# Graph network on 50,000 nodes: target low digits from ScalarE's sign function, late row gathers, run marks stored as rows

## The chip, the cores and the metric

The kernel runs on 1 core of one Trainium2 chip. The metric is device time in microseconds (us) of one launch. The same inputs and outputs hold for both kernels.

## The reference, cut to what matters

```python
def reference(x, src, dst, edge_attr_17, ...):          # x [50000, 96], 25000 edges, sorted by dst
    def L0(x, edge_attr, ...):
        h = relu(edge_attr @ W1.T + b1)
        w = h @ W2.T + b2
        agg = segment_sum(w * x[src], dst, N)
        return relu(x @ Ws.T + bs + agg @ Wn.T + bn)
    def L1(x):                                           # 10 times
        deg_row = maximum(segment_sum(ones, src, N), 1)
        deg_col = maximum(segment_sum(ones, dst, N), 1)
        w = rsqrt(deg_row[src] * deg_col[dst])
        out = segment_sum(out[dst] * w[:, None], src, N) * 0.9 + x * 0.1
    def L2(x):                                           # 16 times, with self-loops
        h = 0.9 * segment_sum(norm * h[row], col, N) + 0.1 * x
    def L3(x):                                           # two graph convolutions with prelu
        ...
    x = layernorm(x + L0(x)); x = layernorm(x + L1(x))
    x = layernorm(x + L2(x)); x = layernorm(x + L3(x))
```

`layernorm` has no affine part. The edges' degrees by source and by target, and the place of each edge in an order by source, depend on the indices alone and are worked out at the start.

## The kernel before

Edges lie in 196 tiles of 128, four tiles to a group, 49 groups of 512 edges (`NT`, `U`, `NGP`, `GE`). The program is a row of blocks with a boundary of all engines between them: `histograms` (L580), `node_records` (L1292), `rank_edges` (L917), `prepare` (L1379), and then `passes` (L1753), the power iteration, the smoothing and the two convolutions. The change touches the first four and the head of the power iteration.

**`histograms`** does three things per group of four tiles, side by side. It counts the edges of each node: a node's number is split in a high digit (196 values) and a low digit (256 values), VectorE writes one-hot rows of each digit (`onehots`, L737 and L738, for target and source, so 16 operations a group), and TensorE multiplies them into two tables in its accumulators (`count`, L812), targets as they come, sources behind the group. ScalarE copies the source table before each group (L908, `snap`) and VectorE stores what rounding lost (`remainder`, L744). Secondly it works out the edge weights: TensorE turns the edge attributes (L820), ScalarE copies them (`copy_edges`, L880), TensorE multiplies (`hide`, L825), ScalarE adds the bias and rectifies (`rectify`, L886), and TensorE multiplies again (`weigh`, L834). Thirdly POOL gathers the rows of x by source (L665, four gathers a group, 196 in all), at most two groups beyond the last that has landed and paced by `remainder`, and VectorE multiplies them by the weights (`gate`, L751). SyncE stores the snapshots and copies x.

The order of ScalarE in the loop is written by hand: snapshot of the counts up to group g, `rectify(g - 1)`, `copy_edges(g)`. TensorE's is: the target counts of tile 0, `weigh(g - 1)`, the target counts of tile 1, the turning of group g's edges, tile 2, tile 3, `hide(g)`, then the source counts of the group. All of it is in order on each engine, so `weigh` holds up what is behind it.

**`node_records`** sums the two tables over the nodes (a running sum, L1348) and writes a record for each node; POOL makes three constants there. **`rank_edges`** gathers records by source (POOL, L988) and by target, places each edge in the order by source (VectorE, L1067 and L1076), sums the gated rows of each run of equal targets (L1125, with the marks of the runs loaded by SyncE and inverted at L1134), and does the first layer. **`prepare`** scatters the edges' records into the order by source, reads them back, works out where runs of equal sources begin (`cont`, L1679 to L1681) and stores these marks to `mask_s` (L1487, four numbers of each partition). Its POOL program ends with four gathers of x rows for the power iteration (`fetch_own`, L564); the first pass fetches the rest.

Of the kernel before, what the change touches and what calls it, by code (L numbers as in the profile page):

```python
# [20 lines left out]
P = 128  # L21
# [28 lines left out]
OWN_FIRST, OWN, OWN_SOON = 124, 8, 4  # L50
# [5 lines left out]
PACE = 2  # L56
# [368 lines left out]
class Program:  # L425
# [130 lines left out]

    def fetch_own(self, pool, tiles):
# [22 lines left out]
    def histograms(self):  # L580
# [4 lines left out]
        with ExitStack() as s:  # L585
# [13 lines left out]
            def part(rows, cols):  # L599
# [26 lines left out]
            const, cleared, onehot, counted, rounded, split, joined = (  # L626
                self.local(f"hist_{n}") for n in ("const", "cleared", "onehot", "counted", "rounded", "split", "joined"))
# [17 lines left out]
            def _(pool):  # L645
# [13 lines left out]
                for g in range(NGP):  # L659
                    if g >= AHEAD_GROUPS:  # L660
                        pool.wait_ge(self.fills(g - AHEAD_GROUPS), self.full(g - AHEAD_GROUPS))
                    if g >= PACE:
                        pool.wait_ge(split, g - PACE + 1)
                    for t in range(g * U, (g + 1) * U):
                        nc.gpsimd.indirect_dma_start(  # L665
                            out=T[:, t * D:(t + 1) * D], out_offset=None, in_=i["x"],
                            in_offset=bass.IndirectOffsetOnAxis(ap=self.src_i[:, t:t + 1], axis=0),
                        ).then_inc(self.fills(g), 16)

            @block.sync  # L670
            def _(sp):
                def load_edge(n):
                    if n >= RE:
                        sp.wait_ge(G["turned"], n - RE + 1)
                    rows = min(GE, E - n * GE) // U
                    sp.dma_start(ea[n % RE][0:rows, :],
                                 i["ea"][n * GE:n * GE + rows * U, :].rearrange("(p u) c -> p (u c)", u=U)
                                 ).then_inc(el[n % RE], 16)

                sp.wait_ge(blank, 3)  # L680
# [40 lines left out]
            def _(dve):  # L721
# [25 lines left out]
                def gate(n):  # L747
                    dve.wait_ge(G["product"], n + 1)
                    dve.wait_ge(self.fills(n), self.full(n))
                    c = slice(n * GD, (n + 1) * GD)  # L750
# [25 lines left out]
                for x in (self.src_i, self.dst_i, next_i):  # L776
                    v.memset(x[:, :], int(PAD)).then_inc(blank, 1)
                link(v.memset(zero[:, :], 0.0))
# [13 lines left out]
                digits(1, self.key_d)  # L792
                dve.wait_ge(const, 4)
# [15 lines left out]
            def _(pe):  # L809
# [63 lines left out]
            def _(act):  # L873
# [13 lines left out]

                act.wait_ge(spread, 1)
# [11 lines left out]
                a_.activation(self.w2[0:D, :], self.bank[5][0:D, 0:D], ACT.Copy).then_inc(set_, 1)  # L900
                for g in range(NGP):
# [6 lines left out]
                    a_.activation(snap[g % SK][:, 0:2 * HW], hist[0], ACT.Copy).then_inc(rounded, 1)  # L908
                    if g:
# [7 lines left out]
    def rank_edges(self):  # L917
# [6 lines left out]
        with ExitStack() as s:  # L924
            def tmp(name, shape, dt=fp32):
# [27 lines left out]
                self.local(f"run_{n}") for n in ("led", "started", "turned", "scanned", "back", "kept"))  # L953
            follows_in = [self.local(f"run_follows{k}") for k in range(2)]
# [13 lines left out]
            def _(pool):  # L968
# [7 lines left out]
                                        fill=0.0, base=0, pattern=[[-1, P]], channel_multiplier=1).then_inc(const, 1)  # L976
                for k, (index, of_, into, groups) in enumerate((
                        (self.src_i, self.meta, self.ms, NGP), (self.dst_i, self.both_t, rows_in, BOTH_FIRST))):
                    if k:
                        pool.wait_ge(met, 16 * MET)  # L980
                    for g in range(groups):
                        q = k * NGP + g
                        if q >= AHEAD_GROUPS:
                            pool.wait_ge(self.fills(q - AHEAD_GROUPS), self.full(q - AHEAD_GROUPS))
                        if q * NT // (NGP + BOTH_FIRST) > PACE * U:
                            pool.wait_ge(nears, q * NT // (NGP + BOTH_FIRST) - PACE * U)
# [69 lines left out]
            def _(dve):  # L1056
# [60 lines left out]

                def run_totals(m):
# [14 lines left out]
                dve.wait_ge(led_in, 16)  # L1133
                v.tensor_scalar(starts, led, -1.0, 1.0, ALU.mult, ALU.add).then_inc(started, 1)  # L1134
                low_digits(0)
                for k in range(LAST):
                    for t in (2 * k, 2 * k + 1):
# [19 lines left out]
            def _(pe):  # L1157
# [34 lines left out]
                def turn_runs(m):  # L1192
                    r = NGP - 1 - m
                    if m >= 2:
# [97 lines left out]
    def node_records(self):  # L1292
        nc = self.nc
        with ExitStack() as s:
# [10 lines left out]
            off = tmp("off", [HP, 1])  # L1305
# [6 lines left out]
            def _(pool):  # L1312
# [7 lines left out]
                               allow_small_or_imprecise_dtypes=True).then_inc(const, 1)  # L1320
            @block.tensor
# [19 lines left out]
            def _(dve):  # L1341
# [3 lines left out]
                for k in range(2):  # L1345
                    dve.wait_ge(turned, k + 1)
                    link(nc.vector.tensor_copy(deg[k][:, :], self.bank[4 + k][0:HP, :]))
                    link(nc.vector.tensor_tensor_scan(out=cum[:, :], data0=ones[:, :], data1=deg[k][:, :], initial=0.0,  # L1348
                                                      op0=ALU.mult, op1=ALU.add))
                    dve.sem_inc(totals, 1)  # L1350
# [1182 lines left out]
```

## Time and profile before

| | us |
|---|---|
| runs | 8792.99, 8794.96 (median), 8802.09 |
| profiled execution | 8794.6 |
| its span, first to last instruction | 8792.5 |
| mean granted clock of TensorE | 0.663 |
| POOL busy in the span | 6478.6 (74%) |
| TensorE busy | 5522.7 (63%) |
| VectorE busy | 4914.3 (56%) |
| ScalarE busy | 2041.9 (23%) |

The profile is of one execution. Engines are PE (TensorE), PEld (its weight loads), DVE (VectorE), ACT (ScalarE), POOL (GpSimd) and SP (SyncE); a `q` behind a name is the engine's queue of instructions, and L744 is line 744 of the kernel. Idle time is put down to what ended it. The granted clock is given as a share of full speed.

In the profiled execution `histograms` runs from 0 to 287 us, `node_records` from 287 to 310, `rank_edges` from 310 to 843, `prepare` from 843 to 1184, and the power iteration follows.

### The profile page before, as it was taken

To read this page: it belongs to the slowest core of one execution; us is meant where nothing else is said; L and a number is where in the kernel's file an instruction comes from. 1 tells how busy PE (TensorE), PEld (TensorE's weight loads), DVE (VectorE), ACT (ScalarE), POOL (GpSimd) and SP (SyncE) were. 2 spreads that over 40 slices of the span, in tenths; PEclk is the share of its full clock that TensorE was granted. 3 is DMA by queue.
4 is the path that set the end of the run, shared out by engine and by line. 5 is a ranking of instruction groups with operands and counts; after the bars stand their busy time and mean duration, and the time that the engine had idled before them with its cause. 6 is when DMAs were issued, how large, how long until landed. Compare 5 with 4: busy or idle time off the path is not lost. (4 is left out here: it accounts for less than half of the span.)

```text
span 8792.5 us, 112510 instructions
## 1 busy us (share of the span) xinstructions
PE 5522.7 (63%) x24034; PEld 4418.1 (50%) x24034; DVE 4914.3 (56%) x12173; ACT 2041.9 (23%) x5604; POOL 6478.6 (74%) x6812
## 2 busy tenths in 40 slices
PE   7676835555555543347777777777776667766643
PEld 6565723333333332226666666656555555655533
DVE  7688736555556566645555555544444444465544
ACT  2355832111111113533111111100000000065433
POOL 6666767777777777677777777777777777777777
PEclk9777855555555555557877777777667666666555
DMA  7665564444444433323444444433333333333211
GB/s 143 130 163 155 148 128 128 113 113 112 113 112 117 115 106 109 110 70 113 121 112 115 114 114 113 113 105 101 96 99 98 98 98 98 103 94 88 81 45 37
DMA packets 955827, 954.11 MB, mean 109 GB/s; under 512 B 426114, under 2 KB 846716, under 8 KB 955046
## 3 DMA queue, kind: packets, MB, share of 16 engines
q1 hardware_dynamic: 696366, 602.87, 22.8%
q0 software_dynamic: 217408, 320.06, 16.7%
q10 hardware_dynamic: 41370, 23.99, 1.1%
q8 instruction: 195, 3.19, 0.1%
q14 instruction: 488, 4.00, 0.1%
HBM read 565.09 MB, written 409.02 MB: 111 GB/s over the span
## 5 line engine op out<-in xcount | busy, mean ns | idle before, releaser
L1996 POOL DMA_INDIRECT l_g<-tab,marks x3094 | 2922.8, 945 | 951.4 <-issue 870.6
L2214 DVE TENSOR_TENSOR_SCAN l_w<-l_m,l_w,bank 96x512 f32<-96x512 bf16 x1248 | 1591.4, 1275 | 2620.5 <-PE bank L2028 2610.7
L2028 PE MATMUL bank<-ident,l_g 128*96 128x128 f32 x5030 | 1165.3, 375 | 1627.7 <-DMA l_g<-tab,marks 914.3
L1996 POOL DMA_INDIRECT l_g<-tab,XM x1740 | 1648.2, 947 | 541.4 <-issue 476.3
L2028 PEld LDWEIGHTS bank<-ident,l_g 128*96 128x96 f32 x5030 | 755.0, 171 | 2073.9 <-DMA l_g<-tab,marks 1030.3
L2048 PEld LDWEIGHTS bank<-ident,l_w 96*128 96x128 f32 x6272 | 1603.7, 328 | 327.9 <-issue 256.4
L2048 PE MATMUL bank<-ident,l_w 96*128 96x96 f32 x6272 | 1508.9, 403 | 10.2 <-DVE l_w L2214 10.2
L2039 PE MATMUL bank<-XM,ident 128*128 128x384 f32 x1568 | 921.4, 681 | 0.0
L2118 ACT ACTIVATE T<-T,marks 128x96 f32<-128x96 f32 x196 | 57.0, 362 | 1967.1 <-DVE T L2239 1966.7
L309 PE MATMUL bank<-tail_xt,v 96*96 96x500 f32 (+1 forms) x298 | 275.7, 1026 | 319.9 <-ACT tail_xt L304 319.9
L420 ACT ACTIVATE tail_y<-bank,tail_of,tail_sc 125x96 f32<-125x96 f32 (+1 forms) x596 | 208.2, 429 | 1095.3 <-DVE tail_of L411 1083.4
L2057 PE MATMUL bank<-ident,l_w 96*128 96x96 f32 x1960 | 402.0, 355 | 36.4 <-DVE l_w L2214 26.6
L2254 DVE TENSOR_TENSOR T<-bank,marks 128x384 f32<-128x384 f32 x735 | 410.1, 558 | 25.6
L2239 DVE TENSOR_TENSOR bank<-bank,T 128x384 f32<-128x384 f32 x735 | 394.5, 537 | 1.3
L2057 PEld LDWEIGHTS bank<-ident,l_w 96*128 96x128 f32 x1960 | 352.4, 226 | 61.3 <-DVE l_w L2214 48.0
L2039 PEld LDWEIGHTS bank<-XM,ident 128*128 128x128 f32 x1568 | 336.6, 265 | 3.9
L400 ACT ACTIVATE tail_sc<-tail_mv,eps_x 125x4 f32<-125x4 f32 (+1 forms) x149 | 44.3, 297 | 1239.8 <-DVE tail_mean L392 1239.8
L1972 POOL DMA_INDIRECT T<-tab,marks x196 | 195.6, 998 | 90.0 <-issue 59.4
L564 POOL DMA_INDIRECT XM<-x1t,XM x196 | 185.4, 946 | 101.9 <-issue 82.7
L988 POOL DMA_INDIRECT meta_s<-meta,src_i x196 | 190.5, 972 | 89.3 <-issue 51.0
L665 POOL DMA_INDIRECT T<-in_x_dram,src_i x196 | 189.7, 968 | 82.7 <-issue 55.1
L1466 POOL DMA_INDIRECT rec<-XM,record_row x196 | 190.8, 973 | 75.5 <-issue 50.0
(334 smaller groups left out, 9352.2 us busy)
## 6 DMA issues: line engine op xcount, KB each, us to landing
tab<-T SPq DMA_DIRECT2D x828, 192.0 KB
row_buffer<-tab ACTq DMA_DIRECT2D x5808, 0.4 KB
tab<-l_o SPq DMA_DIRECT2D x441, 192.0 KB
l_m<-mask_d SPq DMA_DIRECT2D x784, 96.0 KB
l_g<-tab,marks POOLq DMA_INDIRECT x3094
l_m<-mask_s SPq DMA_DIRECT2D x490, 96.0 KB
row_buffer<-tab SPq DMA_DIRECT2D x2640, 0.4 KB
l_g<-tab,XM POOLq DMA_INDIRECT x1740
```

The lines of the kernel that those rows point to most:

```text
L309: return self.nc.tensor.matmul(self.p.bank[5][0:D, 0:w], self.p.v1[0:D, :], self.xt[n % 2][:, 0:w], start=True, stop=True)
L420: last = self.nc.scalar.activation(self.Y[n % 2][0:R, c], self.p.bank[7][0:R, c], ACT.Identity, bias=self.of[n % 2][0:R, u:u + 1], scale=s ...
L1466: nc.gpsimd.indirect_dma_start(out=self.rec[0:TR, :], out_offset=bass.IndirectOffsetOnAxis(ap=row[:, t:t + 1], axis=0), in_=rows_in[:, t, ...
L1972: nc.gpsimd.indirect_dma_start(out=T[:, t * D:(t + 1) * D], out_offset=None, in_=first, in_offset=bass.IndirectOffsetOnAxis(ap=self.own2[: ...
L1996: nc.gpsimd.indirect_dma_start(out=tile(G[q % RG], t), out_offset=None, in_=tables[0:table_at + (2 - p % 2) * TR, :] if p else first, in_o ...
L2028: last = nc.tensor.transpose(a_bank(q)[0:D, u:GE:U], rows[:, u * D:(u + 1) * D], self.ident[:, :])
L2039: nc.tensor.matmul(b_bank(q)[:, 0:GD], self.ident[:, :], group(XS, q % NGP), start=True, stop=False, skip_group_check=True)
L2048: last = nc.tensor.matmul(b_bank(q)[:, u * D:(u + 1) * D], W[q % RW][:, u:GE:U], self.ident[0:D, 0:D], start=False, stop=True, skip_group_ ...
L2057: last = nc.tensor.transpose(b_bank(q)[:, u * D:(u + 1) * D], W[q % RW][:, u:GE:U], self.ident[0:D, 0:D])
L2214: v.tensor_tensor_scan(out=W[q % RW][:, :], data0=masks[q % RM][:, :], data1=a_bank(q)[0:D, :], initial=W[(q - 1) % RW][:, GE - 1:GE] if q ...
L2239: v.tensor_tensor(out=there if p == final else b, in0=b, in1=there, op=ALU.add).then_inc(summed.sem, 1)
L2254: v.tensor_tensor(out=by_row(o), in0=by_row(b), in1=by[:, at].unsqueeze(2).to_broadcast([P, U, D]), op=ALU.mult).then_inc(made.sem, 1)
```

## The change

Three parts, and some that go with them.

- **Target low digits.** VectorE no longer writes the target's low one-hot rows. ScalarE writes the sign of (value − digit + 0.5) for all 256 values instead (`low_steps`), four operations a group, between the snapshot and the rectification. What TensorE sums is then a step, not a spike; `node_records` gets the counts back by halving and by differences. The edges are worked in descending groups, `g = NGP - 1 - n`.
- **Late gathers.** Nine of the 49 groups (`LATE`: 4, 9, ... 44) are gathered later: five of them (20 gathers) in `node_records`, four (16 gathers) at the head of `rank_edges`. Their weights are copied aside in `histograms`, and nine multiplications are made in `rank_edges`. The pace of POOL by `remainder`, and by `nears` in `rank_edges`, is taken out. The inversion of the run marks moves to the second iteration of the ranking loop.
- **Run marks as rows.** In `prepare` TensorE transposes `cont`, VectorE copies it into 49 rows of 512, and `mask_s` is stored from these. The four gathers at the end of `prepare` move to the head of the power iteration.

```diff
-PACE = 2
+LATE = tuple(range(4, NGP, 5))
+SOON = tuple(n for n in range(NGP) if n not in LATE)
+LATE_AT, LATE_FIRST = 12288, 5
...
+    def fetch_sources(self, pool, first, groups):
+        for k, n in enumerate(groups):
+            q, g = first + k, NGP - 1 - n
+            if self.groups + q >= AHEAD_GROUPS:
+                pool.wait_ge(self.fills(q - AHEAD_GROUPS), self.full(q - AHEAD_GROUPS))
+            for t in range(g * U, (g + 1) * U):
+                self.nc.gpsimd.indirect_dma_start(
+                    out=self.T[:, t * D:(t + 1) * D], out_offset=None, in_=self.i["x"],
...
histograms, POOL
-                    if g >= PACE:
-                        pool.wait_ge(split, g - PACE + 1)
...
+                self.fetch_sources(pool, 0, SOON)
...
histograms, VectorE
-                            last = v.tensor_scalar(ol[k][t % R8][:, :], iota_lo[:, :], lo[k][:, t:t + 1], None,
-                                                   ALU.is_equal)
-                        last.then_inc(onehot, 1)
+                        v.tensor_scalar(ol[0][t % R8][:, :], iota_lo[:, :], lo[0][:, t:t + 1], None,
+                                        ALU.is_equal).then_inc(onehot, 1)
...
+                    if n in LATE:
+                        v.tensor_copy(self.late_weights(LATE.index(n)), edge_out[:, 0:GD]).then_inc(G["gated"], 1)
+                        return
...
histograms, TensorE
                         pe.wait_ge(onehot, t + 1)
+                        pe.wait_ge(stepped, t + 1)
                         count(1, t)
...
histograms, ScalarE
+                def low_steps(g):
+                    for t in range(g * U, (g + 1) * U):
+                        a_.activation(ol[1][t % R8][:, :], iota_lo[:, :], ACT.Sign, bias=lo[1][:, t:t + 1]
+                                      ).then_inc(stepped, 1)
...
                     a_.activation(snap[g % SK][:, 0:2 * HW], hist[0], ACT.Copy).then_inc(rounded, 1)
+                    if g + 1 < NGP:
+                        low_steps(g + 1)
                     if g:
                         rectify(g - 1)
...
node_records, POOL
+                self.fetch_sources(pool, len(SOON) - NGP, LATE[0:LATE_FIRST])
...
node_records, VectorE, for the targets
+                        link(v.tensor_copy(tot[:, :], counts[:, LO - 1:M:LO]))
+                        for h in range(2):
+                            link(v.tensor_scalar(end[:, halves[h]], counts[:, halves[h]], tot[:, h:h + 1], 0.5, ALU.add,
+                                                 ALU.mult))
...
rank_edges
+                self.fetch_sources(pool, LATE_FIRST - len(LATE), LATE[LATE_FIRST:])
...
+                    if k == 1:
+                        dve.wait_ge(led_in, 16)
+                        v.tensor_scalar(starts, led, -1.0, 1.0, ALU.mult, ALU.add).then_inc(started, 1)
+                    if 0 <= k - 2 < len(LATE):
+                        gate(k - 2)
...
prepare
-                pool.wait_ge(indexed, 1)
-                self.fetch_own(pool, range(OWN_SOON))
...
-                        sp.dma_start(slots_of(self.mask_s[1:TR + 1]), by_group(cont[:, :])).then_inc(self.order_masked, 16)
+                    sp.wait_ge(rowed, 1)
+                    sp.dma_start(self.mask_s[1:TR + 1].rearrange("(g q) -> g q", q=GE), cont_row[:, :]
+                                 ).then_inc(self.order_masked, 16)
...
+                for u in range(U):
+                    last = nc.tensor.transpose(cont_turn[0:NGP, u:GE:U], cont[:, u:NT:U], self.ident[:, :])
```

ScalarE in the loop of `histograms`, before: the snapshot (L908), the rectification (L886), the edge copy (L880), with the semaphores each waits for in brackets.

```order
L908 ACTIVATE snap<-bank 128x392 [waits hist_kept0,hist_counted]
L886 ACTIVATE XM<-bank,b1a 96x512 [waits edge_product,edge_hidden]
L880 ACTIVATE XM<-bank 68x128 [waits edge_hidden,edge_turned]
L908 ACTIVATE snap<-bank 128x392 [waits hist_kept1,hist_counted]
L886 ACTIVATE XM<-bank,b1a 96x512 [waits edge_product,edge_hidden]
```

The same place in the changed kernel, where L934 is the snapshot, L908 the signs, L904 the rectification and L898 the edge copy.

```order
L934 ACTIVATE snap<-bank 128x392 [waits hist_kept0,hist_counted]
L908 ACTIVATE ol<-iota_lo,XM 128x256 x4
L904 ACTIVATE XM<-bank,b1a 96x512 [waits edge_product,edge_hidden]
L898 ACTIVATE XM<-bank 68x128 [waits edge_hidden,edge_turned]
L934 ACTIVATE snap<-bank 128x392 [waits hist_kept1,hist_counted]
L908 ACTIVATE ol<-iota_lo,XM 128x256 x4
```

Four operations now stand between each snapshot and the rectification behind it, and they wait for nothing of their own.

POOL in the changed kernel at the end of `node_records` and the head of `rank_edges`: L566 is a gather of x rows, L1333 the end of the first block, L998 to L1004 the constants of the second.

```order
L566 DMA T<-in_x_dram,src_i 128x96 [waits group_filled0]
L566 DMA T<-in_x_dram,src_i 128x96 x3
L1333 UNCONDITIONAL_BRANCH
L996 UNCONDITIONAL_BRANCH [waits barrier_Pool_Activation_PE_DVE_SP_gather]
L998 IOTA iota_high 128x196
L1000 IOTA iota_p 128x2
L1002 MEMSET earlier 128x512
L1004 AFFINE_SELECT earlier<-earlier 128x128 [waits rank_const]
L566 DMA T<-in_x_dram,src_i 128x96 [waits group_filled1]
L566 DMA T<-in_x_dram,src_i 128x96 x3
```

The first two rows are the last of five groups of four gathers in `node_records`, the last two the first of four groups in `rank_edges`, which all stand ahead of its first gather of records; before, POOL had no gather in either place.

## Rows read from the trace of the kernel before

**Rows 1.** Summary of waits, 10 to 285 us (total us, times, longest).

```profile
ACT snap L908 <- PE bank L812: 106.5, 46, 3.9
...
PE bank L834 <- ACT XM L886: 45.4, 47, 1.9
DVE T L751 <- PE bank L834: 44.9, 45, 3.1
```

**Rows 2.** Timeline of one group, all engines (start, length, instruction, [idle before]).

```profile
152.33 1.13 PE L834 MATMUL bank<-w2a,XM 97*128 97x96 f32 x8 [0.99 <-ACT XM L886]
...
153.77 0.27 ACT L880 ACTIVATE XM<-bank 68x128 f32<-68x128 f32 x1 [1.50 <-PE bank L820]
...
155.93 0.50 ACT L908 ACTIVATE snap<-bank 128x392 bf16<-128x392 f32 x1 [1.88 <-PE bank L812]
...
156.32 0.67 ACT L886 ACTIVATE XM<-bank,b1a 96x512 f32<-96x512 f32 x1
...
157.05 1.13 PE L834 MATMUL bank<-w2a,XM 97*128 97x96 f32 x8 [0.99 <-ACT XM L886]
```

**Rows 3.** Instruction groups, 0 to 285 us (busy us, mean ns, idle before).

```profile
L738 DVE TENSOR_SCALAR ol<-iota_lo,XM 128x256 bf16<-128x256 bf16 x392 | 116.8, 301 | 0.0
...
L886 ACT ACTIVATE XM<-bank,b1a 96x512 f32<-96x512 f32 x49 | 33.0, 674 | 1.2 <-PE bank L825 1.2
...
L908 ACT ACTIVATE snap<-bank 128x392 bf16<-128x392 f32 x49 | 24.3, 497 | 114.1 <-PE bank L812 106.5 <-DMA snaps<-snap 7.6
```

**Rows 4.** Timeline of ScalarE, 1187 to 1200 us, and one line's instructions there.

```profile
1198.51 1.16 ACT L2108 ACTIVATE l_g<-l_g,XM 128x96 f32<-128x96 f32 x4
...
L2108 ACT ACTIVATE l_g<-l_g,XM x196: 359/364/393, 1187.6 to 1344.2; 128x96 f32<-128x96 f32 x196
```

**Rows 5.** Windows (PE, PEld, DVE, ACT, POOL busy; clock; DMA share; GB/s).

```profile
123.00:198.00 75.00, 58.93 (x526) 51.23 (x525) 61.86 (x271) 21.33 (x48) 57.03 (x60) 1.00 0.70 172
201.00:235.00 34.00, 30.37 (x157) 26.77 (x157) 22.03 (x98) 5.63 (x13) 25.16 (x27) 0.51 0.49 123
310.00:843.00 533.00, 361.85 (x2376) 318.33 (x2376) 441.06 (x2136) 296.91 (x897) 358.73 (x372) 0.76 0.63 159
```

**Rows 6.** Timeline of TensorE, 195 to 206 us: the first matmul after a gap.

```profile
200.39 0.34 PE L812 MATMUL bank<-oh,ol 128*128 128x196 bf16 x2 [2.02 <-DVE ol L738]
```

**Rows 7.** One line's instructions, VectorE L744 over the block, L751 from 205 to 232 us.

```profile
L744 DVE TENSOR_TENSOR snap<-bank,snap x49: 547/554/568, 17.8 to 279.4; 128x392 bf16<-128x392 f32 x49
...
L751 DVE TENSOR_TENSOR T<-bank,T x4: 557/558/558, 209.5 to 231.7; 128x384 f32<-128x384 f32 x4
```

**Rows 8.** Timeline around the node stage and the start of ranking, all engines.

```profile
277.39 1.05 POOL L665 DMA_INDIRECT T<-in_x_dram,src_i  x1 [0.30 <-issue]
...
287.26 0.18 POOL L1313 MEMSET tri<- 98x98 f32 x1 [8.81 <-POOLq L585]
...
309.96 0.30 POOL L969 IOTA iota_high<- 128x196 bf16 x1 [21.66 <-POOLq L1294]
...
323.69 0.42 DVE L1134 TENSOR_SCALAR marks<-marks 128x196 f32<-128x196 bf16 x1 [12.56 <-DMA marks<-mask_d]
```

**Rows 9.** Timeline at the end of `prepare`, and at the end of the first pass.

```profile
1157.44 1.11 POOL L564 DMA_INDIRECT XM<-x1t,XM  x1 [18.31 <-DVEq L1677]
...
1158.51 0.36 SPq L1487 DMA_DIRECT2D mask_s<-cont_s  x1
...
1161.55 0.94 POOL L564 DMA_INDIRECT XM<-x1t,XM  x1 [0.30 <-issue]
...
1183.58 3.60 SPq L2436 DMA_DIRECT2D l_g<-rec  x4
1186.33 0.94 POOL L564 DMA_INDIRECT XM<-x1t,XM  x1 [23.84 <-issue]
...
1345.46 0.94 POOL L564 DMA_INDIRECT XM<-x1t,XM  x1 [0.30 <-issue]
...
1352.91 0.94 POOL L1996 DMA_INDIRECT l_g<-tab,XM  x1 [6.51 <-DMA tab<-l_o]
```

More of the change, by code:

```diff
@@ L1116, in scale_rows, with gate @@
                                            op1=ALU.mult).then_inc(R["scaled"], 1)
+                def gate(k):
+                    q, g = k - len(LATE), NGP - 1 - LATE[k]
+                    dve.wait_ge(self.fills(q), self.full(q))
+                    c = slice(g * GD, (g + 1) * GD)
+                    v.tensor_tensor(out=T[:, c], in0=self.late_weights(k), in1=T[:, c], op=ALU.mult).then_inc(gated, 1)
                 def run_totals(m):
@@ L1354, in _ @@
-                    link(nc.vector.tensor_scalar(end[:, :], cum[:, :], off[:, 0:1], -1.0, ALU.add, ALU.add))
+                    v, counts = nc.vector, self.bank[4 + k][0:HP, :]
+                    if k == 0:
+                        link(v.tensor_copy(deg[k][:, :], counts))
+                        link(v.tensor_tensor_scan(out=cum[:, :], data0=ones[:, :], data1=deg[k][:, :], initial=0.0,
+                                                  op0=ALU.mult, op1=ALU.add))
+                    else:
+                        link(v.tensor_copy(tot[:, :], counts[:, LO - 1:M:LO]))
+                        for h in range(2):
+                            link(v.tensor_scalar(end[:, halves[h]], counts[:, halves[h]], tot[:, h:h + 1], 0.5, ALU.add,
+                                                 ALU.mult))
+                        link(v.tensor_tensor(out=cum[:, M - 1:M], in0=tot[:, 0:1], in1=tot[:, 1:2], op=ALU.add))
@@ new lines, in _ @@
+                    dve.sem_inc(totals, 1)
+                    if k:
+                        upto = end[:, :].rearrange("p (h m) -> p h m", h=2)
+                        each = deg[k][:, :].rearrange("p (h m) -> p h m", h=2)
+                        link(v.tensor_copy(each[:, :, 0:1], upto[:, :, 0:1]))
+                        link(v.tensor_tensor(out=each[:, :, 1:LO], in0=upto[:, :, 1:LO], in1=upto[:, :, 0:LO - 1],
+                                             op=ALU.subtract))
+                    dve.wait_ge(offs, k + 1)
@@ new lines, in _ @@
+                    link(v.tensor_copy(off[:, :], self.bank[2 + k][0:HP, 0:1]))
+                    if k == 0:
+                        link(v.tensor_scalar(end[:, :], cum[:, :], off[:, 0:1], -1.0, ALU.add, ALU.add))
+                    else:
+                        link(v.tensor_copy(both[:, 0:1], off[:, :]))
+                        link(v.tensor_tensor(out=both[:, 1:2], in0=off[:, :], in1=tot[:, 0:1], op=ALU.add))
+                        for h in range(2):
+                            link(v.tensor_scalar(end[:, halves[h]], end[:, halves[h]], both[:, h:h + 1], -1.0, ALU.add,
+                                                 ALU.add))
@@ L1483, in order_out @@
                 def order_out():
-                    sp.wait_ge(linked, 1)
-                    with nc.allow_non_contiguous_dma(reason="four numbers of each partition"):
-                        sp.dma_start(slots_of(self.mask_s[1:TR + 1]), by_group(cont[:, :])).then_inc(self.order_masked, 16)
+                    sp.wait_ge(rowed, 1)
+                    sp.dma_start(self.mask_s[1:TR + 1].rearrange("(g q) -> g q", q=GE), cont_row[:, :]
+                                 ).then_inc(self.order_masked, 16)
                 with nc.allow_non_contiguous_dma(reason="one number"):
@@ L1897, in own_tiles @@
             def own_tiles(p):
-                return range(OWN_FIRST + (p - 1) * OWN if p else OWN_SOON, OWN_FIRST + p * OWN)
+                return range(OWN_FIRST + (p - 1) * OWN if p else 0, OWN_FIRST + p * OWN)
             def own_count(k, end):
```

69 lines of the change are left out of this document (37 added, 32 removed).

## The prediction, made before the changed kernel had run

> **What bounds the kernel now.** I read the summary of waits first, because the change works on one block and the question is who waits for whom there. In the histogram block ScalarE's snapshot waits 46 times for TensorE's source counts, and TensorE's `weigh` (L834) waits 47 times for ScalarE's rectification (L886). VectorE in turn waits 45 times for TensorE, 44.9 us in all, some 0.9 us a group [rows 1]. So TensorE and ScalarE form the loop, and VectorE stands outside it with time to spare.
>
> One group in the timeline shows the loop closed [rows 2]. The snapshot starts at 155.93, behind 1.88 us of waiting for the source counts, the rectification at 156.32, and `weigh` at 157.05, after 0.99 us in which TensorE did nothing. From `weigh` to `weigh` is 157.05 − 152.33 = 4.72 us. ScalarE has idle time in the group, 1.50 us before the copy of edges and 1.88 us before the snapshot, but none between snapshot and rectification.
>
> The windows show the same block at both clock levels [rows 5]: a granted clock of 1.00 (the upper level, 2.4 GHz) from 123 to 198 us, and 0.51 (the lower, 1.2 GHz) from 201 to 235 us. Before the fall TensorE had waited 2.02 us, ending at 200.39 [rows 6]. Gaps of 0.99 us, one a group, had not made it fall. At the lower level a group takes (231.7 − 209.5) / 3 = 7.40 us. The 48 intervals of the block run from 17.8 to 279.4 us, so their mean is 5.45 us and their sum 261.6 us [rows 7]. At 4.72 us throughout it would be 226.6 us.
>
> **The sign operations.** VectorE loses four `L738` instructions of 0.301 us in each group [rows 3]. I cost that at nothing, since VectorE already waits for TensorE [rows 1]. ScalarE gains four operations of 128x256, placed between snapshot and rectification, in the one stretch of its order where TensorE waits. Over the whole block the rectification itself waited only 1.2 us [rows 3], so what stands ahead of it delays it in full. The trace has no sign operation. The nearest is a one-pointer activation of 128x96: one takes 0.364 us, four in a row 1.16 us [rows 4], so each further one costs (1.16 − 0.364) / 3 = 0.265 us. A column costs (0.497 − 0.27) / (392 − 128) = 0.00086 us between the edge copy's 128 columns (0.27 us) [rows 2] and the snapshot's 392 [rows 3]. For 256 columns that makes 0.265 + 160 × 0.00086 = 0.40 us, or 1.60 us a group. The lower bound is column time alone, 256 × 0.00086 × 4 = 0.88 us; the upper bound is no overlap at all, 4 × (0.364 + 0.138) = 2.0 us. I take 1.60, which is nearest to the row of the same form.
>
> The Trainium skill prices this differently: "ScalarE: Activation LUTs", section "ACT is a hardware spline evaluator", gives 0.833 ns an element whatever the function, and "Perfetto Trace Analysis", section "Optimizing Scalar/DVE Operations", some 93 ns of overhead for an operand in SBUF. As an estimate from these pages, four signs are 4 × (0.213 + 0.093) = 1.23 us, 18 us less over the block than by the row. For the 96 columns of the row the pages would give 0.173 us where the trace has 0.265 us, so the trace disagrees on the overhead and I keep the row.
>
> A group becomes 4.72 + 1.60 = 6.32 us at the upper clock and 7.40 + 1.60 = 9.00 us at the lower, and TensorE's wait grows from 0.99 to about 2.6 us in every group, above the 2.02 us after which the clock fell [rows 6]. Over 48 intervals: all upper 303 us (+42), today's mix 261.6 + 77 (+77), all lower 432 us (+170). Since each group now holds such a gap I expect more time at the lower level than today, but not all of it: ranking, where TensorE is 0.68 busy, has a mean granted clock of 0.76 [rows 5]. I take the middle between +77 and +170, **+123 us**. The bounds are +42 (bare column time and today's mix) and 48 × (7.40 + 2.0) − 262 = +190.
>
> **The gathers.** POOL issues a gather every 0.94 + 0.30 = 1.24 us [rows 9], 5.0 us a group of four. Taking 36 of 196 out of the histogram block, and its wait for VectorE, gives nothing, as POOL's gathers follow the loop and not the other way. In the node stage POOL is idle from 288.30 for 21.66 us [rows 8]; 20 gathers there end at 288.3 + 25 = 313.3. At the last boundary POOL began again 8.81 us behind its last gather [rows 8], which puts ranking's start at 322.1 instead of 309.96: **+12 us**. Bounds: +3 with nothing behind the gather, and +24 with the 21 us that separate 1162.5 and 1183.58 at the end of `prepare` [rows 9].
>
> Ranking is VectorE's stage, 441 of 533 us busy [rows 5]. It gains nine multiplications of 0.557 us [rows 7], 5 us. The wait of 12.56 us for the run marks at its start [rows 8] moves one iteration on; the first scan needs a second load from the same queue, so I count only 3 us of it back. POOL's 16 further gathers, 20 us, fit beside its 359 us of work in 533 [rows 5]. Net **+2 us**, between −8 (the whole wait comes back) and +15 (the gathers ahead of the first records delay VectorE by half their 20 us).
>
> **Run marks as rows.** `mask_s` is issued at 1158.51 and the next block starts at 1183.58, 25 us later [rows 9]. In the change it is 49 rows of 1 KB behind four transposes and a copy, and POOL's four gathers of 1157.44 to 1162.49 [rows 9] leave the block. With the 8.8 us of the boundary in [rows 8] behind 1158.5 the next block starts near 1167.3, some 16 us earlier. The four gathers come back at the head of the pass, 5 us, but its own rows ended at 1346.4 while the wait that ended the pass lasted until 1352.91 [rows 9], so 6.5 us cover them. Without that cover 5 us return. **−16 us**, between −12 (the transposes, the copy and the transfer take 4 us more) and −20 (they overlap the boundary, and VectorE's remaining work too).
>
> The recovery of counts in the node stage replaces one scan by a few tensor operations of similar length, beside POOL's 25 us of gathers: nothing. If those were shorter, VectorE's chain, which ended the stage before, would be late next.
>
> **Sum.** +123 + 12 + 2 − 16 = +121 us, against the profiled execution's 8794.6 us (span 8792.5 and 2.1 around it; the median of the runs is 8795.0, the same for this purpose). Forecast **8915 us**.
>
> **Rivals.**
> - *The clock stays up.* The loop is longer but TensorE's level holds at 1.00: 303 us, +42, and with the other terms (+12 + 2 − 16 = −2), 8794.6 + 40 = 8835 us. For it: 75 us at 1.00 in the block with a gap in every group [rows 5]. Against it: the fall right behind 2.02 us [rows 6]. The Trainium skill, "TensorE: Matmul & The Clock Gate", section "Why this matters for your kernels", names idle gaps between bursts of matmuls as what lowers the clock, and by its measure the gaps forecast here are too short for that; the trace speaks against it with that one fall. 0.14.
> - *Neutral.* The signs cost only their 0.88 us and the clock stays up: 48 × (4.72 + 0.88) = 269 us, +7 − 2, 8800 us. 0.08.
> - *Faster: VectorE was what broke the loop.* Today's 35 us above 226.6 would come from late one-hots, as in the gap of [rows 6], which ended on `L738`. With 12 in place of 16 VectorE is never late, the clock never falls, and the signs run in ScalarE's 1.50 and 1.88 us of idle time [rows 2]: 226.6 us, −35 − 2, 8758 us. It decides as soon as less than some 0.4 us of each group's 1.60 stay on the loop at the upper clock. Against it: VectorE's 44.9 us of waiting [rows 1], and the order in which the signs stand behind the snapshot that TensorE's counts release. 0.11.
> - *The change does not do what it says.* The listing of ScalarE's order shows the signs, and POOL's the moved gathers, so nothing is left for this.
>
> **The numbers.** The forecast case holds 0.62, from 8870 (today's mix, +77, and little from the rest) to 8970. Above that, 0.05. The range 8825 to 8970 holds this case and the rival with the clock up, 0.76, and some of what lies between. About 0.2% (17.6 us) is what a measurement of this kernel can tell from no change. Faster 0.11, same 0.08, slower 0.81.
>
> **What would show it.** Four sign operations between snapshot and rectification with a pitch near 0.40 us; TensorE's wait at `weigh` near 2.6 us and a total over 100 us where 45.4 stood; group intervals of 6.3 or 9.0 us and a lower granted clock in the first 400 us; a node stage of some 35 us; a `mask_s` transfer of a few us. I am wrong if the signs start before the snapshot, if the clock stays at 1.00, or if `weigh` then waits for something other than ScalarE.

## The result and the profile after

The changed kernel takes 8949.55 us in the median (8948.06 to 8951.09), the kernel before 8794.96. The ratio is 1.0174, with a 95% interval of 1.0151 to 1.0197: slower by some 154 us. The forecast was 8915 us in a range of 8825 to 8970. The span of the profiled execution is 8946.3 us against 8792.5.

Where the 153.8 us arose is read from the first instruction of each block in the two timelines:

| block | before, us | after, us | change | forecast |
|---|---|---|---|---|
| `histograms` | 287.3 | 443.0 | +155.8 | +123 |
| `node_records` | 22.7 | 31.0 | +8.3 | +12 |
| `rank_edges` | 532.7 | 534.8 | +2.1 | +2 |
| `prepare`, to the next block's first load | 340.9 | 322.6 | −18.3 | −16 |
| from there to the first gather of the second step | 169.3 | 170.0 | +0.7 | 0 |
| all behind it | 7439.6 | 7444.9 | +5.3 | 0 |

The summary of waits, 10 to 442 us of the changed kernel (total us, times, longest), answers to [rows 1]:

```profile
ACT snap L934 <- PE bank L829: 161.6, 48, 3.5
DVE T L765 <- PE bank L851: 133.3, 39, 3.7
...
PE bank L851 <- ACT XM L904: 117.0, 48, 2.6
```

TensorE's wait for the rectification, here L904, went from 45.4 to 117.0 us over nearly as many groups. VectorE, from which work was taken, waits 133.3 us for TensorE where it waited 44.9.

One group in the timeline answers to [rows 2]:

```profile
156.78 2.02 PE L851 MATMUL bank<-w2a,XM 97*128 97x96 f32 x8 [2.42 <-ACT XM L904]
...
159.38 0.27 ACT L898 ACTIVATE XM<-bank 68x128 f32<-68x128 f32 x1 [2.65 <-PE bank L837]
...
163.07 0.50 ACT L934 ACTIVATE snap<-bank 128x392 bf16<-128x392 f32 x1 [3.42 <-PE bank L829]
...
163.47 1.69 ACT L908 ACTIVATE ol<-iota_lo,XM 128x256 bf16<-128x256 bf16 x4
...
165.06 0.67 ACT L904 ACTIVATE XM<-bank,b1a 96x512 f32<-96x512 f32 x1
...
165.78 2.02 PE L851 MATMUL bank<-w2a,XM 97*128 97x96 f32 x8 [2.42 <-ACT XM L904]
```

Snapshot to rectification was 0.39 us and is now 165.06 − 163.07 = 1.99, so the four signs add 1.60 us. From `weigh` to `weigh` is 9.00 us. ScalarE still has 2.65 and 3.42 us of idle time in the group, in other places.

The length of one sign, and the remainder's first and last start (the groups by line, 0 to 445 us, and one line's instructions):

```profile
L908 ACT ACTIVATE ol<-iota_lo,XM 128x256 bf16<-128x256 bf16 x196 | 82.8, 496 | 4.4 <-DVEq L809 4.4
...
L754 DVE TENSOR_TENSOR snap<-bank,snap x49: 551/567/568, 17.1 to 435.7; 128x392 bf16<-128x392 f32 x49
```

A sign takes 0.496 us, and 48 intervals take 435.7 − 17.1 = 418.6 us where they took 261.6 [rows 7].

The windows show the granted clock (columns as in [rows 5]):

```profile
20.00:40.00 20.00, 14.89 (x80) 13.09 (x78) 8.35 (x34) 6.26 (x16) 15.16 (x16) 1.00 0.50 121
40.00:60.00 20.00, 13.31 (x66) 11.49 (x66) 9.82 (x37) 7.89 (x20) 15.14 (x16) 0.56 0.53 130
...
45.00:430.00 385.00, 276.36 (x1446) 246.39 (x1444) 150.61 (x625) 128.85 (x308) 125.80 (x132) 0.58 0.45 90
```

And TensorE's timeline, the third and fourth group and then the last one, ahead of whose products no signs stand (L842 are the hidden products, L851 the weight products):

```profile
36.76 1.94 PE L842 MATMUL bank<-XM 68*96 68x128 f32 x8
38.49 1.24 PE L829 MATMUL bank<-oh,ol 128*128 128x196 bf16 x10
42.31 1.99 PE L851 MATMUL bank<-w2a,XM 97*128 97x96 f32 x8 [2.58 <-ACT XM L904]
...
436.25 1.13 PE L851 MATMUL bank<-w2a,XM 97*128 97x96 f32 x8 [0.99 <-ACT XM L904]
...
438.02 1.11 PE L842 MATMUL bank<-XM 68*96 68x128 f32 x8
```

The kernel before, in its first group and in the middle of the block (L825 are the hidden products):

```profile
18.28 1.91 PE L825 MATMUL bank<-XM 68*96 68x128 f32 x8
...
149.38 1.11 PE L825 MATMUL bank<-XM 68*96 68x128 f32 x8
```

The clock column alone would say that the clock fell at 42 us, behind a gap of 2.58 us. The lengths of the products say otherwise. Eight hidden products take 1.94 us ahead of that gap as well, and the weight products that start at 24.75 and 33.75 us take 2.02 us; both are the lengths of the lower level, 1.2 GHz, although the column reads 1.00 there.

The kernel before shows the same: the column reads 1.00 from 20 to 50 us, while the hidden products take 1.94 us until 47.9 us and 1.11 us from 54.1 us on. So in the kernel before the products reached the upper level some 50 us into the block; in the changed kernel the hidden products keep 1.94 us in every group until the signs end, and only the last group, with a wait of 0.99 us, has 1.11.

Over the 385 us from 45 us on the mean granted clock is 0.58, near the lower level. It is not 0.50 because the upper level comes back eighteen times between 66 and 421 us, for less than 4 us each, and mostly while TensorE waits: from 66.5 to 69.5 us the clock is 1.00 and TensorE is busy for 0.42 of the 3.0 us.

The other blocks, from the timelines of all engines:

```profile
443.04 0.18 POOL L1353 MEMSET tri<- 98x98 f32 x1 [224.79 <-POOLq L603]
...
470.42 0.95 POOL L566 DMA_INDIRECT T<-in_x_dram,src_i  x1 [0.30 <-issue]
474.00 0.29 POOL L998 IOTA iota_high<- 128x196 bf16 x1 [2.64 <-POOLq L1333]
...
490.52 1.22 DVE L1159 TENSOR_TENSOR_SCAN marks<-marks,bank 96x512 f32<-96x512 bf16 x1 [10.68 <-DMA marks<-mask_d]
...
1325.98 0.29 SPq L1547 DMA_DIRECT2D mask_s<-cont_row  x1
1331.37 4.63 SPq L2502 DMA_DIRECT2D l_g<-rec  x7
...
1500.10 0.95 POOL L582 DMA_INDIRECT XM<-x1t,XM  x1 [0.30 <-issue]
1501.35 0.94 POOL L2062 DMA_INDIRECT l_g<-tab,XM  x1 [0.30 <-issue]
```

POOL's last late gather ends the node stage: the next block begins 2.64 us behind it. The forecast took 8.81 us from the end of `histograms` for this. There VectorE was still at work when POOL had ended:

```profile
284.32 0.56 DVE L751 TENSOR_TENSOR T<-bank,T 128x384 f32<-128x384 f32 x1 [3.10 <-PE bank L834]
```

Its last multiplication ends at 284.88 us, and the node stage starts at 287.26 [rows 8], so only 2.4 of the 8.81 us lie behind the last instruction of the block.

The store of run marks is followed by the next block in 1331.37 − 1325.98 = 5.4 us, where 25 us lay between them [rows 9]. The last fetch of the first pass is followed by the first gather of the next step without a wait, where POOL had waited 6.51 us.

### The profile page after: what moved, and what is told of

Read it like the earlier page. It is cut to its first block and busy times, and to the rows that moved or that the text cites. A ratio compares the mean times of both kernels' runs of the same rounds, so it can differ in the third digit from the quotient of the medians.

```text
span 8946.3 us, 112604 instructions
## 1 busy us (share of the span) xinstructions
PE 5628.9 (63%) x24038; PEld 4518.1 (51%) x24038; DVE 4881.9 (55%) x11996; ACT 2121.3 (24%) x5800; POOL 6486.2 (73%) x6812
## 5 line engine op out<-in xcount | busy, mean ns | idle before, releaser
L566 POOL DMA_INDIRECT T<-in_x_dram,src_i x196 | 189.1, 965 | 70.8 <-issue 57.6
L374 PE MATMUL bank<-ident,tail_up 96*125 96x96 f32 (+1 forms) x396 | 93.1, 382 | 232.6 <-DVE tail_up L364 232.6
```

## The experiments

The theory: four signs a group lie on the loop of TensorE and ScalarE because they stand ahead of the rectification, and the longer gap lets the clock fall, which costs the rest. The rivals: the signs or the step counts cost as much anywhere; the clock has another cause; the late gathers and what belongs to them cost the time. The runs fell into three sets, each beside the kernel before on its own chip: 8795.5 us for the first four kernels, 8804.1 for the next four, 8796.2 for the last two. So ratios and block lengths are compared. These are the lengths from the profiled executions:

| run | mean interval, us | `histograms` | node stage | ranking | `prepare` | ratio to before |
|---|---|---|---|---|---|---|
| before | 5.45 | 287.3 | 22.7 | 532.7 | 340.9 | 1 |
| changed | 8.72 | 443.0 | 31.0 | 534.8 | 322.6 | 1.0174 [1.0151, 1.0197] |
| signs behind the edge copy | 5.02 | 265.4 | 31.1 | 533.1 | 323.9 | 0.9968 [0.9954, 0.9982] |
| gap filled | 6.32 | 329.9 | 31.2 | 537.3 | 322.6 | 1.0033 [1.0021, 1.0046] |
| six signs | 9.68 | 490.9 | 31.0 | 531.5 | 325.1 | 1.0219 [1.0201, 1.0236] |
| one-hots on VectorE | 5.19 | 274.0 | 31.4 | 534.7 | 324.0 | 0.9974 [0.9961, 0.9986] |
| run marks alone | 5.44 | 285.7 | 22.4 | 535.3 | 323.5 | 0.9984 [0.9975, 0.9993] |
| rectification first | 4.52 | 242.6 | 31.2 | 539.4 | 323.1 | 0.9945 [0.9930, 0.9961] |
| before, rectification first | 5.18 | 276.8 | 22.7 | 531.1 | 340.9 | 0.9993 [0.9984, 1.0002] |
| late gathers in ranking | 4.42 | 237.6 | 23.2 | 537.6 | 324.7 | 0.9932 [0.9917, 0.9947] |
| the same once more | 4.50 | 240.6 | 23.2 | 539.3 | 322.5 | 0.9923 [0.9906, 0.9939] |
| and signs before the rectification | 4.36 | 234.6 | 23.2 | 534.0 | 324.8 | 0.9921 [0.9904, 0.9937] |

**The signs moved into ScalarE's idle time.**

```diff
                     a_.activation(snap[g % SK][:, 0:2 * HW], hist[0], ACT.Copy).then_inc(rounded, 1)
-                    if g + 1 < NGP:
-                        low_steps(g + 1)
                     if g:
                         rectify(g - 1)
                     copy_edges(g)
+                    if g + 1 < NGP:
+                        low_steps(g + 1)
```

> The changed kernel with the four signs of a group moved behind the copy of edges, into ScalarE's wait for the next snapshot; nothing else differs. Theory (the signs cost what they hold up between snapshot and rectification): groups return to 4.7 us where the clock is up, the counting block to 227 to 262 us from some 419, so 8757 to 8793 us. Rival A (a sign operation, the step counts or the copies aside cost the time wherever they stand): within 20 us of 8950. Rival B (1.88 us of waiting does not hold four signs, the snapshot becomes late): in between, 8820 to 8900, with TensorE waiting for the remainder instead of the rectification.

Measured: 8770.76 us, as the theory said. The same four signs now cost nothing. ScalarE's timeline:

```profile
142.29 1.69 ACT L908 ACTIVATE ol<-iota_lo,XM 128x256 bf16<-128x256 bf16 x4
144.27 0.50 ACT L934 ACTIVATE snap<-bank 128x392 bf16<-128x392 f32 x1 [0.29 <-PE bank L829]
```

They run in the wait ahead of the snapshot and leave 0.29 us of it; the next snapshot follows 4.72 us later, at 148.99, the interval of the kernel before at the upper level. One move of a line is worth 179 us, so rival A falls.

**The gap filled.** Twelve products of zeros on TensorE ahead of each `weigh`, into an unused accumulator.

```diff
                         if t % U == 0 and g:
+                            for _ in range(12):
+                                nc.tensor.matmul(self.bank[5][:, 0:2 * HW], zeros[:, 0:P], zeros[:, 0:2 * HW],
+                                                 start=True, stop=True)
                             weigh(g - 1)
```

> The changed kernel with twelve idle multiplications of zeros on TensorE in each group, in the gap ahead of the second weight product, into an accumulator that nothing reads. Theory (some 77 us are the signs on the loop, and the other 79 us the clock that falls because of the gap): the granted clock stays at 1.00, a group takes 6.3 to 6.6 us, the block 303 to 320 us, so 8834 to 8850 us, faster although TensorE does more. Rival (the clock is low for another reason, or the signs cost all of it): the clock stays at 0.5, twelve products of some 0.33 us outlast the gap by about 1.3 us a group, some 9010 us.

Measured: 8828.88 us, 121 us less than the changed kernel, though TensorE does more and ScalarE's order is the same. TensorE's timeline and the window:

```profile
150.38 2.15 PE L877 MATMUL bank<-zeros 128*128 128x392 bf16 x12
153.12 1.13 PE L851 MATMUL bank<-w2a,XM 97*128 97x96 f32 x8 [0.59 <-ACT XM L907]
...
25.00:320.00 295.00, 265.70 (x2100) 203.95 (x2099) 160.13 (x668) 135.54 (x324) 141.50 (x149) 1.00 0.64 125
...
L754 DVE TENSOR_TENSOR snap<-bank,snap x49: 551/567/568, 17.9 to 321.4; 128x392 bf16<-128x392 f32 x49
```

The gap is 0.59 us instead of 2.42, the granted clock 1.00 over 295 us (the hidden products take 1.11 us from 27.8 us on, so the column is right here), and a mean interval is (321.4 − 17.9) / 48 = 6.32 us, the forecast's figure for the upper clock. The total lies 5 us below what was expected, because the passes behind took 8 us less than in the changed kernel. This parts the two costs: with 226.6 us for 48 groups of 4.72, the signs make it 303.5 (+77) and the lower clock 418.6 (+115). The kernel before stood at 261.6 us, since part of its own block ran at the lower level, so 157 of these 192 us are new.

**Six signs.** Two more a group, into tiles that nothing reads.

```diff
                     for t in range(g * U, (g + 1) * U):
+                        if t % U < 2:
+                            a_.activation(again[g % 2 * 2 + t % U][:, :], iota_lo[:, :], ACT.Sign,
+                                          bias=lo[1][:, t:t + 1]).then_inc(stepped, 1)
```

> The changed kernel with two more signs a group, the same operation into a tile that nothing reads. Theory: each sign lies on the loop with 0.40 us, so 48 x 2 x 0.40 = 38 us more, 8988 us. Rival (only the clock, or the first sign's start, costs time): 8945 to 8955 us.

Measured: 8990.48 us, 41 us more than the changed kernel. In ScalarE's timeline the first signs of a group follow each other by 0.40 us:

```profile
151.75 0.50 ACT L910 ACTIVATE again<-iota_lo,XM 128x256 bf16<-128x256 bf16 x1
152.15 0.50 ACT L912 ACTIVATE ol<-iota_lo,XM 128x256 bf16<-128x256 bf16 x1
```

The interval grew by 0.96 us instead of 0.80. The trace shows the rest: a group that lies wholly at the lower level takes 9.80 us here (hidden products at 177.48 and 187.28 us) and 9.00 us in the changed kernel, which is the 0.80, and the short returns of the upper level shorten fewer groups, every seventh here (9.47 us) and most of them in the changed kernel (8.4 to 8.9 us).

**One-hots back on VectorE.** The first part of the change undone, the other two kept.

```diff
                         for k in (1, 0):
                             v.tensor_scalar(oh[k][t % R8][:, :], iota_hi[:, :], hi[k][:, t:t + 1], None, ALU.is_equal)
-                        v.tensor_scalar(ol[0][t % R8][:, :], iota_lo[:, :], lo[0][:, t:t + 1], None,
-                                        ALU.is_equal).then_inc(onehot, 1)
+                            last = v.tensor_scalar(ol[k][t % R8][:, :], iota_lo[:, :], lo[k][:, t:t + 1], None,
+                                                   ALU.is_equal)
+                        last.then_inc(onehot, 1)
...
-                    if g + 1 < NGP:
-                        low_steps(g + 1)
```

> The changed kernel without its first part: VectorE writes the target's low one-hot rows again and the node stage sums them as before; late gathers, order of groups and run marks as in the change. Theory: the block falls to 227 to 262 us, total 8758 to 8793 us, that is the kernel before with the node stage 8 us longer and the end of the fourth block 18 us shorter. Rival A (late gathers, copies aside or the order of groups cost the time): near 8950. Rival B (VectorE's load held the loop before): no faster than 8790.

Measured: 8774.08 us, within what was expected. The late gathers, the copies aside and the descending groups do not cost the time; the first part alone does, 169 us of `histograms`. TensorE waits for the rectification as it did before:

```profile
PE bank L850 <- ACT XM L902: 47.1, 47, 2.0
```

Against the signs in ScalarE's idle time it takes 3 us more, which is within the intervals of the two ratios. So at that length of the loop, no gain from moving one-hots off VectorE can be told.

**The run marks alone**, on the kernel before.

```diff
-                    sp.wait_ge(linked, 1)
-                    with nc.allow_non_contiguous_dma(reason="four numbers of each partition"):
-                        sp.dma_start(slots_of(self.mask_s[1:TR + 1]), by_group(cont[:, :])).then_inc(self.order_masked, 16)
+                    sp.wait_ge(rowed, 1)
+                    sp.dma_start(self.mask_s[1:TR + 1].rearrange("(g q) -> g q", q=GE), cont_row[:, :]
+                                 ).then_inc(self.order_masked, 16)
```

> The kernel before with the third part alone: run marks transposed on TensorE, copied and stored as 49 rows of 1 KB. The four gathers of rows at the end of the fourth block stay there. Theory (the 25 us between the store and the next block were the store's 6272 descriptors, which also slowed the boundary): the next block starts 14 to 18 us earlier, 8777 to 8782 us. Rival (POOL's gathers and its 8.8 us at the boundary bound the end of the block, or the later wait for the first pass hides it): no more than 5 us, 8790 to 8796 us.

Measured: 8792.17 us beside 8804.07, a gain of 14 us by the ratio (6 to 22). The total in us is outside the theory's range and inside the rival's, because both were set from 8795; `prepare` shrank by 17.4 us, which is the theory's. From SyncE's timeline:

```profile
1161.40 0.29 SPq L1488 DMA_DIRECT2D mask_s<-cont_row  x1
...
1167.02 5.47 SPq L2444 DMA_DIRECT2D l_g<-rec  x7
```

With POOL's four gathers still there, the next block starts 5.6 us behind the store. So the store by single numbers made some 19 of the 25 us, and moving the gathers brought no more than 1 us.

**The rectification first.** Its line moves from behind the next snapshot to behind the copy of edges; the signs stay where the change has them.

```diff
                     if g + 1 < NGP:
                         low_steps(g + 1)
-                    if g:
-                        rectify(g - 1)
                     copy_edges(g)
-                rectify(NGP - 1)
+                    rectify(g)
```

> The changed kernel with ScalarE's rectification of a group moved from behind the next snapshot to right behind the copy of edges, with the signs where the change put them. Theory (the signs cost only because TensorE waits for the rectification behind them): TensorE's wait for the rectification disappears, the clock stays up, a group takes some 4.0 us, TensorE's own 3.75 us and little more, the block 192 to 205 us, and the total 8720 to 8745 us, faster than the kernel before and than the move of the signs alone. Rival (four signs keep ScalarE too busy: the copy of edges becomes late and TensorE waits for it): a group of 4.7 us or more, 8760 us or more.

Measured: 8759.48 us, 0.9945 of before, faster than both kernels. That it is faster than the move of the signs is shown by the block (242.6 us against 265.4) and not by the totals, whose intervals touch. It is 15 us above the range, of which 9 are the chip's slower kernel before. TensorE's and ScalarE's timeline:

```profile
160.09 1.13 PE L851 MATMUL bank<-w2a,XM 97*128 97x96 f32 x8
...
162.32 1.11 PE L842 MATMUL bank<-XM 68*96 68x128 f32 x8 [0.49 <-ACT XM L898]
...
163.48 0.68 ACT L904 ACTIVATE XM<-bank,b1a 96x512 f32<-96x512 f32 x1 [1.20 <-PE bank L842]
...
164.21 1.13 PE L851 MATMUL bank<-w2a,XM 97*128 97x96 f32 x8
```

`weigh` no longer waits, and a group takes 164.21 − 160.09 = 4.12 us. Part of the rival holds too: the signs now delay the copy of edges, and TensorE waits 0.49 us ahead of the hidden product. The mean over the block is 4.52 us, since the first eighteen intervals take 93 us and not 74; so the 192 to 205 us were missed by 12 (48 intervals took 217.0).

**The kernel before, rectification first.** The same move, without the change.

```diff
-                    if g:
-                        rectify(g - 1)
                     copy_edges(g)
-                rectify(NGP - 1)
+                    rectify(g)
```

> The kernel before with the same move of the rectification and nothing else. Theory (without the wait for ScalarE, VectorE's sixteen one-hots, 4.15 us of work a group, or POOL's four gathers, 5.0 us, set the pace): a group takes 4.2 to 5.0 us, the block 245 to 255 us from the 262 of before, 8778 to 8790 us; moving work off VectorE is worth something only then. Rival (TensorE's wait was the whole bound): groups of 4.0 us, 8725 to 8745 us, as with the signs on ScalarE.

Measured: 8799.40 us beside 8804.07, no difference that can be told, though the block is 10 us shorter in the profiled execution. The summary of waits, and POOL at the end of the block:

```profile
PE bank L812 <- DVE ol L738: 47.8, 38, 7.8
DVE T L751 <- DMA T<-in_x_dram,src_i: 42.3, 20, 7.8
...
276.85 0.18 POOL L1311 MEMSET tri<- 98x98 f32 x1 [8.81 <-POOLq L585]
```

The wait for ScalarE is replaced by waits for VectorE's one-hots (11.0 us before) and for POOL's gathers (7.8 before). So with the rectification first the change has something to give: signs on ScalarE and fewer gathers in the block together are worth 276.8 − 242.6 = 34 us of `histograms`. How they divide between the two was not tried.

**All late gathers in ranking**, on the run with the rectification first.

```diff
-LATE_AT, LATE_FIRST = 12288, 5
+LATE_AT, LATE_FIRST = 12288, 0
```

> The kernel with the rectification ahead of the snapshot, and all 36 late gathers at the head of the third block, none in the node stage. Theory (the node stage became 8 us longer because POOL's 20 gathers outlast VectorE there): the node stage returns to 22.7 us, and the third block has room for 45 us more of gathers, 4 to 8 us less than the run with the rectification ahead. Rival (POOL's further gathers delay the third block): the same time or up to 10 us more.

> The run with all late gathers in the third block once more, beside the one with the signs moved, on the same chip: a ratio of 0.991 to 0.995 to the kernel before, as in its first run.

Measured: 8745.59 us beside 8804.07, and 8732.11 beside 8796.24, ratios of 0.9932 and 0.9923. POOL at the two ends of the node stage:

```profile
237.59 0.18 POOL L1351 MEMSET tri<- 98x98 f32 x1 [17.17 <-POOLq L603]
...
260.80 0.30 POOL L996 IOTA iota_high<- 128x196 bf16 x1 [22.16 <-POOLq L1331]
```

The stage takes 23.2 us, 8.0 less, and ranking no more than before the move. The intervals of the two totals overlap, so it is the stage that shows it.

**The signs moved once more**, between the copy of edges and the rectification.

```diff
-                    if g + 1 < NGP:
-                        low_steps(g + 1)
                     copy_edges(g)
+                    if g + 1 < NGP:
+                        low_steps(g + 1)
                     rectify(g)
```

> The run with all late gathers in the third block, and with the signs moved once more, from behind the snapshot to between the copy of edges and the rectification. Theory (what TensorE still waits there, 0.49 us a group ahead of the hidden product, is the signs ahead of the copy of edges): that wait goes, a group falls from 4.12 to 3.7 to 3.9 us where the clock is up, the block from 238 to 215 to 228 us, 10 to 22 us off. Rival (the rectification becomes late by as much, or VectorE or POOL's 5.0 us for four gathers hold the loop): no more than 5 us off, or slower.

Measured: 8727.31 us, 0.9921 of before, the lowest time of the study, but not to be told from the 0.9923 of the run beside it. TensorE's timeline:

```profile
152.15 1.13 PE L851 MATMUL bank<-w2a,XM 97*128 97x96 f32 x8 [0.20 <-ACT XM L904]
...
153.93 1.11 PE L842 MATMUL bank<-XM 68*96 68x128 f32 x8
...
156.10 1.13 PE L851 MATMUL bank<-w2a,XM 97*128 97x96 f32 x8 [0.21 <-ACT XM L904]
```

The 0.49 us are gone, 0.20 us appear at `weigh`, and a group takes 3.95 us at the upper clock. The block is 6 us shorter than in the run beside it (3 us than in that kernel's first run), of 10 to 22 expected, so the theory's range was missed.

## Why the prediction was right, and where a term was off

The direction and the mechanism held, and the time lies in the range. By its steps:

- **The price of a sign.** 0.40 us by the activation of 96 columns and the column's slope; measured 0.40 us from start to start and 1.60 us a group. The estimate worked out from figures of the Trainium skill's pages ("ScalarE: Activation LUTs", section "ACT is a hardware spline evaluator", and "Perfetto Trace Analysis", section "Optimizing Scalar/DVE Operations") was 1.23 us a group, too low by 0.37, so the measurement decides for the row.
- **Its place.** On the loop, as forecast: 117.0 us of waiting at `weigh`, and the same signs cost nothing behind the copy of edges.
- **The clock, the term that was mis-sized.** "I take the middle between +77 and +170" assumed that part of the block would stay at the upper level. The products had the lengths of the lower level from the first group until the signs ended, and the upper level came back only for short stretches, mostly waits; so the 48 intervals took 418.6 us, +157 instead of +123, close to the +170 of a block that is low throughout. The prediction looked for a fall behind a long gap; what the runs show is that the gap, one in every group, kept the clock from coming up, as it had some 50 us into the block before. The 34 us are as much as the whole miss of the forecast; that the other terms cancel, among them 5.3 us that none of them forecast, is luck. The argument from ranking's mean clock did not carry. The filled gap shows the cause: with 0.59 us in place of 2.42 the products were at the upper level's length from 27.8 us on.
- **The rival with the clock up** was 8835 us, worked out from rows. The filled gap gave 8829 us, which is its condition brought about. In the changed kernel gaps of 2.4 to 2.6 us, one a group, were enough to keep the granted clock at 0.58 on average. So the trace speaks against the rule that the prediction took from the Trainium skill's page "TensorE: Matmul & The Clock Gate", section "Why this matters for your kernels", by which such gaps are too short to lower the clock.
- **The node stage.** +12 forecast, +8.3 measured. The gathers ended at 471.4 us, 28 us behind the block's start, instead of 26; what was off is the boundary, 2.64 us behind POOL's last gather instead of the 8.81 that I had carried over from `histograms`. For 6.4 of those 8.81 us other engines of the block were still at work, so it was not the price of a boundary.
- **Ranking**, +2 against +2.1. The wait for the run marks is still there, 10.68 us ahead of the first scan instead of 12.56 ahead of the first operation, and nine multiplications of some 0.56 us came in. The agreement to 0.1 us says little: the same block took 531.5 to 539.4 us in the kernels with the late gathers, and 531.1 to 535.3 us in the three without them.
- **Run marks**, −16 against −18.3, and alone −17.4 in `prepare`. The cover for the four gathers held: POOL's 6.51 us of waiting became 0.3, and the pass is 0.7 us longer.
- **Behind that**, 5.3 us that no step forecast. The passes behind differ by as much where the program is the same: 7436.4 to 7441.8 us among the first four experiments, and 7452.8 and 7440.5 us for the kernel with all late gathers in ranking, in its two sets. So the 5.3 us are not put down to the change.

That VectorE waited for TensorE spoke rightly against the change. What the prediction did not see is the next step, that one other line in ScalarE's order, the place of the rectification, decides whether TensorE waits for VectorE's one-hots at all: 11.0 us before, 47.8 us with the rectification first.

## What to carry to other kernels

Before work is moved to an idle engine, look where in that engine's order it lands: ScalarE was busy for 21 of 75 us [rows 5], yet four signs ahead of the one operation that TensorE waits for cost 1.60 us a group each time, and nothing behind the copy of edges, where ScalarE waited anyway. Here a recurring wait of TensorE that grew from 1.0 us to 2.4 kept the lower clock for nearly the whole loop, and that cost more (115 us) than the signs on the loop (77 us), both against a loop at the upper level throughout; so where such a wait grows, a forecast should price the whole loop at either level. Taking work off an engine gave nothing that could be told as long as that engine waited for the loop. And read the clock column beside the length of one kind of product: ahead of the first change that the trace holds, the two disagreed here.

## What was not expected of the hardware

Products of zeros made the kernel faster by 121 us: TensorE's granted clock stayed at 1.00 for 295 us with them, where it was 0.58 over 385 us without. In the changed kernel TensorE was busy for 276.4 of 385 us and the clock came back only for less than 4 us at a time; in the kernel before it came back after some 34 us, in which TensorE was busy for 30.4 us [rows 5], so that some 0.8 us a group were idle. The time between POOL's last gather and the next block was 8.81 us in two kernels whose gathers ran to the end of `histograms` ([rows 8] and the kernel before with the rectification first) and 9.28 us in a third (the run marks alone), while behind the gathers of the node stage it was 2.64 us. Behind the last work of any engine in those three blocks it was 2.4, 5.5 and 1.7 us; what sets these was not tried.
